# A fused four-layer kernel: five of 32 scan products on another engine, a third home for the states, paired router products

## The chip, the cores and the metric

The kernel is one program on one core of a Trainium2 chip. The metric is the device time in microseconds (us) of one execution. Before the change it was 1005.11 us, the median of three runs (1002.9 to 1006.55). The profiled execution took 1004.66 us.

## The reference

A residual stream `x` of 1024 tokens by 256 features passes eight blocks, each added with a gate. The first is a selective state space model on the context; the fourth and the eighth are mixtures of experts with a router in front.

```python
# block 1: per batch, 256 channels e, 16 states n
u = silu(conv(in_proj_w @ ctx) + conv_b)
delta = softplus(dt_proj_w @ dt_lo + dt_proj_b);  A = -exp(A_log)
def step(state, (d_t, B_t, C_t, u_t)):
    dA = exp(d_t[..., None] * A)
    state = state * dA + (d_t * u_t)[..., None] * B_t[:, None, :]
    return state, einsum('ben,bn->be', state, C_t)
y = (ys + D * u) * silu(z)                     # z = layernorm(x)
x = x + tanh(g0) * y
x = x + tanh(g1) * ffn_ternary_weights_int8_activations(layernorm(x))
x = x + tanh(g2) * attention_16_heads(layernorm(x), ctx)
x = x + tanh(g3) * moe(layernorm(x))           # logits = x @ gate_w.T, top 4 of 16, and a shared expert
x = x + tanh(g4) * map_attention;  x = x + tanh(g5) * hadamard_ffn
x = x + tanh(g6) * map_attention;  x = x + tanh(g7) * moe   # top 2 of 8
```

## The kernel before

The tokens are worked on as two halves of 512 (`HALF`), half `h` being batches 2h and 2h+1. The program is written out by hand for each engine, in the order `ORDER = ["M", "F0", "A1", "F"]`: the state space block, the quantised feed-forward block, the attention with 16 heads for each half, and then the three last feed-forward blocks with the two map attentions woven in between (tables of places, `beside`). Engines meet at semaphores, each named after what it counts.

**The scan.** There are 32 rounds `g`, one per state (16) and half (2). A round needs, for 256 channels (two groups `e` of 128) and 512 tokens:

- ScalarE copies the broadcast row B from PSUM to one of three tiles `m_Bs` (`copy_B`, L889) and makes dA = exp(delta * A) into PSUM banks 6 and 7, one exponential for each `e` (L1002). The exponential of `e` waits for the scan of the round before that read the bank. The copy of B for round g+2 stands between the two exponentials of round g.
- GpSimd makes dBu = du * B (L2057), into one of two tiles.
- VectorE runs the scan itself, state * dA + dBu, once for each `e` (L1480), and writes it into a state tile (`hst`, two tiles: `m_h` and `m_inv`). Then it makes the product with C for the round before (L1486), from the state tile and PSUM bank 3 into one of two tiles `m_hC`.
- TensorE broadcasts B (L466, bank 2) and C (L494, bank 3) from a split row, and sums the products into y, banks 0 and 1, by products with the identity (L500, four matrix instructions for a round). In TensorE's queue a round reads: B for g+3; the wait for product g-1; C for g; the sums of product g-1; in some rounds a product of value weights (L511, rounds 0, 2, ... 14 and 22 to 29).

So the next C is asked for once the last product is read, the next B stands behind the sums, and the second exponential behind the copy of B. Further work is dropped into chosen rounds: the rounding of quantised weights on ScalarE (`ROUND_AT`), the gate of half 0 at round 17 (`gated(0)`, L1466), the residual at 20 (L1351), statistics at 21 (L1315 to L1329), scales at 24 (L1520), maxima at 27 (L1511), rounded values at 30 (L1526) on VectorE, and three steps on delta of half 1 on GpSimd behind rounds 3, 6 and 9 (`delta1`).

**The end of the scan.** TensorE's queue ends with C for round 31, the sums of product 30, eight transposes of the quantised rows (L531), the sums of product 31, and the first gate and up products of the next block (L557). Their result goes through Silu on ScalarE (L1072) to VectorE (L1555).

**The router.** The activations and the router's weights are each kept as a high and a low part (`x_norm_T_hi`, `x_norm_T_lo`, `r_w_hi`, `r_w_lo`). `mm3` (L434 to L436) adds three products: high by high, high by low, low by high. `router_logits` calls it for each tile of 128 tokens (4 per half) and each half of the features (2), with the activations as the weights that are loaded and 32 columns of router weights passing. It runs for two blocks and two halves. VectorE takes the logits with one copy (L1614).

## Time and profile before

| | before |
|---|---|
| median of three runs | 1005.11 us |
| the profiled execution | 1004.66 us |
| its span in the profile | 1002.9 us |
| TensorE (PE) busy | 912.1 us, 91% |
| VectorE (DVE) busy | 715.4 us, 71% |
| ScalarE (ACT) busy | 642.6 us, 64% |
| GpSimd (POOL) busy | 492.7 us, 49% |

The span is the time from the first to the last instruction in the profile, and the busy times are shares of it. They are averages over stages: in the page's 40 slices VectorE is at 9 tenths in the second to sixth slice, and TensorE from the eleventh on. The page also gives the clock that TensorE was granted, in tenths of full speed (PEclk), slice by slice.

In the names of the profile a state tile `m_inv` is the second home of the states, and `m_split` a tile that splits the rows of B and C before the scan. Numbers behind tile names are left out in the profile, and stand in the listings of order below.

### The profile page before, as it was taken

What the parts mean: (1) busy time and instruction counts of PE and PEld (TensorE: products, weight loads), DVE (VectorE), ACT (ScalarE), POOL (GpSimd) and SP (SyncE); (2) the same over time, 40 slices, a digit from 0 to 9 for tenths busy, and PEclk for the clock granted to TensorE, in tenths of its full rate; (3) what the DMA queues carried; (4) which work ended last, traced back from release to release, by engine and by line L of the source; (5) the groups of instructions that cost most, each with busy time, mean ns of one, the idle gap of its engine ahead of it and who ended that gap; (6) DMA issues with size and microseconds to landing.
All of it is one profiled execution on the core that took longest, in us unless ns stands there. A gap on an engine that the chain in (4) does not pass through costs nothing.

```text
span 1002.9 us, 15717 instructions
## 1 busy us (share of the span) xinstructions
PE 912.1 (91%) x5336; PEld 747.2 (75%) x5336; DVE 715.4 (71%) x1303; ACT 642.6 (64%) x1246; POOL 492.7 (49%) x488
## 2 busy tenths in 40 slices
PE   6477677668999999999989999999999999999998
PEld 2133233346999999999968888888888888888887
DVE  6899998986777777777667675796666655666544
ACT  5767765766777777777655666756667544554553
POOL 1487561126766666666443443454344544444442
PEclk8599989798999999999999999999999999999999
DMA  9200100003000000000019511211112500021221
GB/s 346 115 1 0 63 1 0 1 1 159 1 2 2 1 1 1 1 2 1 1 51 339 181 53 46 61 64 54 46 58 56 232 1 1 1 74 53 62 65 45
DMA packets 17612, 56.26 MB, mean 56 GB/s; under 512 B 3073, under 2 KB 4201, under 8 KB 15389
## 3 DMA queue, kind: packets, MB, share of 16 engines
q1 hardware_dynamic: 5341, 34.27, 9.0%
q10 hardware_dynamic: 12192, 20.98, 7.1%
q8 instruction: 44, 0.72, 0.3%
q14 instruction: 35, 0.29, 0.1%
HBM read 54.08 MB, written 1.16 MB: 55 GB/s over the span
## 4 chain that ended last, share of the span: by engine, by line
PE 50%; DVE 13%; POOL 8%; issue 7%; ACT 3%; ACTq 1%; DMA 1%; DVEq 0%; POOLq 0%
PE psum L434 14%; PE psum L436 14%; PE psum L435 14%; POOL a_P L2020 3%; DVE a_max L1718 2%; POOL a_rk L1941 2%; POOL a_rq L1949 2%; DVE psum L1654 1%; PE psum L843 1%; DVE psum L1854 1%; PE psum L769 1%; PE psum L700 1%; DVE bn_st L1315 1%; PE psum L803 1%; ACT L1133 1%
## 5 line engine op out<-in xcount | busy, mean ns | idle before, releaser
L434 PE MATMUL psum<-x_norm_T_hi,f_wgu_hi 128*128 128x512 f32 x400 | 160.3, 401 | 3.2 <-DVE f_h_lo L1861 3.2
L436 PE MATMUL psum<-x_norm_T_hi,f_wgu_lo 128*128 128x512 f32 x400 | 157.5, 394 | 0.0
L435 PE MATMUL psum<-x_norm_T_lo,f_wgu_hi 128*128 128x512 f32 x400 | 156.8, 392 | 0.0
L434 PE MATMUL psum<-f_wd_hi,f_h_hi 128*128 128x256 f32 x400 | 121.9, 305 | 0.1
L1654 DVE TENSOR_TENSOR psum<-f_silu,psum 128x512 f32<-128x512 f32 x100 | 69.3, 693 | 69.5 <-PE psum L436 47.2
L436 PE MATMUL psum<-f_wd_hi,f_h_lo 128*128 128x256 f32 x400 | 112.9, 282 | 0.0
L435 PE MATMUL psum<-f_wd_lo,f_h_hi 128*128 128x256 f32 x400 | 112.9, 282 | 0.0
L1861 DVE TENSOR_TENSOR f_h_lo<-psum,f_h_hi 128x512 fp32r<-128x512 f32 x100 | 68.9, 689 | 51.6 <-ACT f_h_hi L889 51.1
L1954 POOL TENSOR_TENSOR f_wgu_lo<-f_w,f_wgu_hi 128x512 fp32r<-128x512 f32 x44 | 56.7, 1290 | 94.3 <-ACT f_wgu_hi L889 94.3
L1954 POOL TENSOR_TENSOR f_wgu_lo<-f_wb,f_wgu_hi 128x512 fp32r<-128x512 f32 x36 | 46.6, 1293 | 103.5 <-ACT f_wgu_hi L889 103.5
L2057 POOL TENSOR_TENSOR m_dBu<-m_du,m_Bs 128x1024 f32<-128x1024 f32 x31 | 73.0, 2355 | 35.1 <-DVE m_inv L1480 16.1
L2020 POOL TENSOR_TENSOR a_P<-a_P,a_row_inv 128x1024 f32<-128x1024 f32 x32 | 60.6, 1894 | 59.6 <-DVE a_row_inv L1755 59.6
L434 PEld LDWEIGHTS psum<-x_norm_T_hi,f_wgu_hi 128*128 128x128 f32 x400 | 75.6, 189 | 17.4 <-issue 3.9
L436 PEld LDWEIGHTS psum<-x_norm_T_hi,f_wgu_lo 128*128 128x128 f32 x400 | 75.0, 188 | 17.2
L435 PEld LDWEIGHTS psum<-x_norm_T_lo,f_wgu_hi 128*128 128x128 f32 x400 | 75.7, 189 | 13.2
L1133 ACT ACTIVATE f_silu<-psum 128x512 f32<-128x512 f32 x100 | 59.7, 597 | 38.5 <-PE psum L436 38.3
L434 PEld LDWEIGHTS psum<-f_wd_hi,f_h_hi 128*128 128x128 f32 x400 | 76.0, 190 | 5.3 <-issue 2.2
L435 PEld LDWEIGHTS psum<-f_wd_lo,f_h_hi 128*128 128x128 f32 x400 | 76.2, 191 | 4.6 <-issue 1.9
L436 PEld LDWEIGHTS psum<-f_wd_hi,f_h_lo 128*128 128x128 f32 x400 | 76.2, 190 | 0.0
L889 ACT ACTIVATE a_PT_hi<-psum 128x1024 fp32r<-128x1024 f32 x32 | 32.8, 1025 | 62.1 <-PE psum L769 62.1
L889 ACT ACTIVATE f_h_hi<-psum 128x512 fp32r<-128x512 f32 x100 | 58.7, 587 | 19.9 <-DVE psum L1854 19.8
L1228 ACT ACTIVATE a_P<-psum,a_neg_max,a_rq 128x256 f32<-128x256 f32 x128 | 70.7, 574 | 0.4 <-DVE a_neg_max L1722 0.4
(328 smaller groups left out, 2635.1 us busy)
## 6 DMA issues: line engine op xcount, KB each, us to landing
f_cw<-r_rows ACTq DMA_DIRECT2D x38, 256.0 KB, 3.3
f_wb<-in_f1b SPq DMA_DIRECT2D x6, 1152.0 KB, 9.7
f_w<-in_f3w SPq DMA_DIRECT2D x1, 5376.0 KB, 16.6
f_wa<-in_f1a SPq DMA_DIRECT2D x1, 3840.0 KB, 11.8
w_raw<-in_w0raw SPq DMA_DIRECT2D x1, 3072.0 KB, 14.9
f_w<-in_f2w SPq DMA_DIRECT2D x2, 1536.0 KB, 8.6
f_cw<-r_rows ACTq DMA_DIRECT2D x12, 224.0 KB, 3.0
f_cw<-r_rows ACTq DMA_DIRECT2D x12, 192.0 KB, 2.9
```

What stands on the lines that cost most here:

```text
L434: mm(out, wh, xh, start=start, stop=False, **kw)
L435: mm(out, wh, xl, start=False, stop=False, **kw)
L436: return mm(out, wl, xh, start=False, stop=stop, **kw)
L889: return A(out_, in_, ACT.Copy)
L1133: A(sg[g % 2][:, :], ps[:, 2 + 2 * (g % 2), :], ACT.Silu).then_inc(S("f_sg"), 1)
L1228: last = A(Pm[i % 2][:, t, :], ps[:, 2 + t // 2, (t % 2) * DM:(t % 2 + 1) * DM], ACT.Exp, bias=nb[:, t:t + 1], scale=rq[i % 2][:, t:t + 1] ...
L1654: V.tensor_tensor(ps[:, 2 + 2 * (g % 2), :], sg[g % 2][:, :], ps[:, 3 + 2 * (g % 2), :], ALU.mult).then_inc(S("f_m"), 1)
L1718: link(V.tensor_reduce(mx[:, :], ps[:, 2:4, :].rearrange("p a (b n) -> p (a b) n", b=2), AX, ALU.max))
L1861: V.tensor_tensor(hl[g % 2][:, :], ps[:, 2 + 2 * (g % 2), :], hh[g % 2][:, :].bitcast(f32), ALU.subtract).then_inc(S("f_hl"), 1)
L1954: G.tensor_tensor(wgl[g % 2][:, :], raw_w(l, j)[:, 0:GU], wgh[g % 2][:, :].bitcast(f32), ALU.subtract).then_inc(S("f_wg"), 1)
L2020: G.tensor_tensor(Pm[i % 2][:, :, :], Pm[i % 2][:, :, :], bc(ri[:, :].unsqueeze(2), [P, TH, DM]), ALU.mult).then_inc(S("a_pn"), 1)
L2057: G.tensor_tensor(dBu[g % 2][:, :, :], du[g // NS][:, :, :], bc(Bs[g % 3][:, :].unsqueeze(1), [P, 2, HALF]), ALU.mult).then_inc(S("m_dBu"), 1)
```

## The change

Four things change.

1. The states get a third tile, `m_split`, which is free during the scan. Round g uses tile g % 3 up to round 28, and after that two tiles in turn, since the quantised rows are written over `m_split` in round 30. The scan of round g waits for product g-3, where it waited for product g-2.
2. In rounds 10, 13, 16, 19 and 22 GpSimd makes the product with C, behind the dBu of two rounds later. It can't read the PSUM bank, so ScalarE copies C to a tile (`m_tap_w`) in those rounds. VectorE skips these products. TensorE and the scans wait for the right count of both engines' products (`products_done`).
3. The end of the scan: the transposes of the quantised rows stand before the wait for product 30 in TensorE's queue, and ScalarE issues a Silu on one element behind the copy of the transposes, so that the table is loaded there.
4. The router: high and low parts of the weights lie side by side, so that one product of 64 columns gives high by high and high by low, and a second of 32 columns adds low by high. VectorE adds the two parts of the logits in two instructions.

Beside these the `delta1` steps stand behind rounds 3, 5 and 7, and `ROUND_AT` names other rounds.

```diff
-    hst = [hst0, zinv]
+    hst = [hst0, zinv, spl]
+    POOL_ROUNDS = (10, 13, 16, 19, 22)
+    Cs = tapw.rearrange("p a b -> p (a b)")
+    def products_done(eng, n):
+        by_pool = sum(1 for r in POOL_ROUNDS if r < n)
+        if n > by_pool:
+            eng.wait_ge(S("m_hC"), n - by_pool)
+        if by_pool:
+            eng.wait_ge(S("m_hC_pool"), by_pool)
+    LAST_OF_THREE = NS + 12
+    def state_home(g):
+        return g % 3 if g <= LAST_OF_THREE else (g + 1) % 2
...
+                if g == NS + 15:
+                    loaded(pe, "identb")
+                    pe.wait_ge(S("wvo_copied"), HEADS - 1)
+                    quantised_inputs(0)
                 if g:
-                    pe.wait_ge(S("m_hC"), g)
+                    products_done(pe, g)
...
-                    last = mm3(ps[:, 7, t * 32:(t + 1) * 32], xh[:, c, sl], xl[:, c, sl], wrh[:, c, :], wrl[:, c, :],
-                               c == 0, c == KC - 1)
+                    mm(ps[:, 7, t * 64:(t + 1) * 64], xh[:, c, sl], wrs[:, c, :, :].rearrange("p a n -> p (a n)"), start=c == 0, stop=False,
+                       skip_group_check=True)
+                    last = mm(ps[:, 7, t * 64:t * 64 + 32], xl[:, c, sl], wrs[:, c, 0, :], start=False, stop=c == KC - 1, skip_group_check=True)
...
-            ROUND_AT = [9, 11, 13, 15] + list(range(17, 25))
+            ROUND_AT = [9, 10, 12, 13, 15, 16, 18, 19, 21, 22, 24, 25]
...
+                if g - 1 in POOL_ROUNDS:
+                    if g - 1 > POOL_ROUNDS[0]:
+                        act.wait_ge(S("m_hC_pool"), POOL_ROUNDS.index(g - 1))
+                    act.wait_ge(S("m_C"), g)
+                    copy(Cs[:, :], ps[:, 3, :]).then_inc(S("m_Ccopy"), 1)
...
             quantised_inputs(0)
+            A(scratch[:, 22:23], epsc[:, :], ACT.Silu)
...
-                    if g >= 2:
-                        dve.wait_ge(S("m_hC"), g - 1)
+                    if g >= 3:
+                        products_done(dve, g - 1 if g > LAST_OF_THREE else g - 2)
...
-                        V.tensor_tensor_scan(hst[g % 2][:, e, :], ps[:, 6 + e, :], dBu[g % 2][:, e, :], 0.0, ALU.mult, ALU.add).then_inc(S("m_h"), 1)
-                if g:
+                        V.tensor_tensor_scan(hst[state_home(g)][:, e, :], ps[:, 6 + e, :], dBu[g % 2][:, e, :], 0.0, ALU.mult, ALU.add).then_inc(S("m_h"), 1)
+                if g and g - 1 not in POOL_ROUNDS:
...
-            V.tensor_copy(rl[:, :, 0:nl], ps[:, 7, 0:TH * 32].rearrange("p (t n) -> p t n", t=TH)[:, :, 0:nl]).then_inc(S("b7_free"), 1)
+            parts_ = ps[:, 7, 0:TH * 64].rearrange("p (t n) -> p t n", t=TH)
+            link(V.tensor_copy(rl[:, :, 0:nl], parts_[:, :, 32:32 + nl]))
+            V.tensor_tensor(rl[:, :, 0:nl], parts_[:, :, 0:nl], rl[:, :, 0:nl], ALU.add).then_inc(S("b7_free"), 1)
...
-                    if g in (3, 6, 9):
-                        delta1(g // 3 - 1)
+                    if g in (3, 5, 7):
+                        delta1((g - 3) // 2)
+                    r = g - 2
+                    if r in POOL_ROUNDS:
+                        pool.wait_ge(S("m_h"), 2 * (r + 1))
+                        pool.wait_ge(S("m_y"), r - 1)
+                        pool.wait_ge(S("m_Ccopy"), POOL_ROUNDS.index(r) + 1)
+                        G.tensor_tensor(hC[r % 2][:, :, :], hst[state_home(r)][:, :, :], bc(Cs[:, :].unsqueeze(1), [P, 2, HALF]),
+                                        ALU.mult).then_inc(S("m_hC_pool"), 1)
```

In the listings of the program's order a line names the instruction, its output and inputs; a scan reads SCALAR_TENSOR_TENSOR with the state tile as its output. GpSimd's queue from the dBu of round 10 on, before:

```order
L2057 TENSOR_TENSOR m_dBu0_116<-m_du0_113,m_Bs1_119 128x1024 [waits m_h,m_du,m_Bcopy]
L2057 TENSOR_TENSOR m_dBu1_117<-m_du0_113,m_Bs2_120 128x1024 [waits m_h,m_du,m_Bcopy]
L2057 TENSOR_TENSOR m_dBu0_116<-m_du0_113,m_Bs0_118 128x1024 [waits m_h,m_du,m_Bcopy]
L2057 TENSOR_TENSOR m_dBu1_117<-m_du0_113,m_Bs1_119 128x1024 [waits m_h,m_du,m_Bcopy]
L2057 TENSOR_TENSOR m_dBu0_116<-m_du0_113,m_Bs2_120 128x1024 [waits m_h,m_du,m_Bcopy]
```

and in the changed kernel:

```order
L2085 TENSOR_TENSOR m_dBu0_115<-m_du0_112,m_Bs1_118 128x1024 [waits m_h,m_du,m_Bcopy]
L2085 TENSOR_TENSOR m_dBu1_116<-m_du0_112,m_Bs2_119 128x1024 [waits m_h,m_du,m_Bcopy]
L2085 TENSOR_TENSOR m_dBu0_115<-m_du0_112,m_Bs0_117 128x1024 [waits m_h,m_du,m_Bcopy]
L2094 TENSOR_TENSOR m_hC0_121<-m_inv1_125,m_tap_w_156 128x1024 [waits m_Ccopy,m_y,m_h]
L2085 TENSOR_TENSOR m_dBu1_116<-m_du0_112,m_Bs1_118 128x1024 [waits m_h,m_du,m_Bcopy]
L2085 TENSOR_TENSOR m_dBu0_115<-m_du0_112,m_Bs2_119 128x1024 [waits m_h,m_du,m_Bcopy]
L2085 TENSOR_TENSOR m_dBu1_116<-m_du0_112,m_Bs0_117 128x1024 [waits m_h,m_du,m_Bcopy]
L2094 TENSOR_TENSOR m_hC1_122<-m_inv1_125,m_tap_w_156 128x1024 [waits m_Ccopy,m_y,m_h]
```

A product with C now stands behind the dBu of round 12 and again behind that of round 15. VectorE's queue from the scans of round 15 to those of round 18, before:

```order
L1480 SCALAR_TENSOR_TENSOR m_inv1_126<-psum,m_dBu1_117 128x512 x2
L1486 TENSOR_TENSOR m_hC0_122<-m_h_121,psum 128x1024
L1480 SCALAR_TENSOR_TENSOR m_h_121<-psum,m_dBu0_116 128x512 x2
L1486 TENSOR_TENSOR m_hC1_123<-m_inv1_126,psum 128x1024
L1480 SCALAR_TENSOR_TENSOR m_inv1_126<-psum,m_dBu1_117 128x512 x2
L1486 TENSOR_TENSOR m_hC0_122<-m_h_121,psum 128x1024
L1466 TENSOR_TENSOR m_u0_111<-psum,x_norm0_50 128x512 x2
L1480 SCALAR_TENSOR_TENSOR m_h_121<-psum,m_dBu0_116 128x512 x2
```

and in the changed kernel, from the scans of round 16 on:

```order
L1506 SCALAR_TENSOR_TENSOR m_inv1_125<-psum,m_dBu0_115 128x512 x2
L1512 TENSOR_TENSOR m_hC1_122<-m_h_120,psum 128x1024
L1506 SCALAR_TENSOR_TENSOR m_split_109<-psum,m_dBu1_116 128x512 x2
L1492 TENSOR_TENSOR m_u0_110<-psum,x_norm0_50 128x512 x2
L1506 SCALAR_TENSOR_TENSOR m_h_120<-psum,m_dBu0_115 128x512 x2
```

The product of round 16 is gone from between the scans of round 17 and the gate, and three tiles take turns. TensorE's queue at the end of the scan, before, from C for round 30 to the first gate product:

```order
L494 MATMUL psum<-m_bc_split1_125,sel_bc_152 128x512
L500 MATMUL psum<-m_hC1_123,ident_f_60 128x512 x2
L494 MATMUL psum<-m_bc_split1_125,sel_bc_152 128x512
L500 MATMUL psum<-m_hC0_122,ident_f_60 128x512 x2
L531 MATMUL psum<-ident_b_61,q_x0_134 128x128 x8
L500 MATMUL psum<-m_hC1_123,ident_f_60 128x512 x2
L557 MATMUL psum<-w0_quant0_147,q_xT0_137 128x512 x2
```

and in the changed kernel:

```order
L517 MATMUL psum<-m_bc_split1_124,sel_bc_152 128x512
L523 MATMUL psum<-m_hC1_122,ident_f_60 128x512 x2
L550 MATMUL psum<-ident_b_61,q_x0_133 128x128 x8
L517 MATMUL psum<-m_bc_split1_124,sel_bc_152 128x512
L523 MATMUL psum<-m_hC0_121,ident_f_60 128x512 x2
L523 MATMUL psum<-m_hC1_122,ident_f_60 128x512 x2
L576 MATMUL psum<-w0_quant0_146,q_xT0_136 128x512 x2
```

The eight transposes moved ahead of the last C; the sums of products 30 and 31 follow each other.

## Rows read from the trace of the kernel before

**Rows 1.** Busy time by stage: start:end, length, then PE, PEld, DVE, ACT, POOL, PEclk.
```profile
47.00:165.00 118.00, 84.70 (x221) 36.06 (x221) 113.33 (x115) 80.47 (x129) 76.44 (x34) 0.93 0.04 14
...
258.00:525.00 267.00, 261.53 (x1977) 247.38 (x1976) 189.47 (x334) 195.13 (x483) 170.30 (x205) 1.00 0.02 5
525.00:1003.00 478.00, 468.69 (x2683) 406.19 (x2682) 302.88 (x630) 274.56 (x490) 202.76 (x203) 1.00 0.24 79
```

**Rows 2.** Timeline of VectorE in the scan: start, length, instruction.
```profile
88.70 2.34 DVE L1480 TENSOR_TENSOR_SCAN m_inv<-psum,m_dBu 128x512 f32<-128x512 f32 x2
90.96 1.20 DVE L1486 TENSOR_TENSOR m_hC<-m_h,psum 128x1024 f32<-128x1024 f32 x1
92.24 2.34 DVE L1480 TENSOR_TENSOR_SCAN m_h<-psum,m_dBu 128x512 f32<-128x512 f32 x2
...
105.12 1.20 DVE L1486 TENSOR_TENSOR m_hC<-m_h,psum 128x1024 f32<-128x1024 f32 x1
106.23 1.28 DVE L1466 TENSOR_TENSOR m_u<-psum,x_norm 128x512 f32<-128x512 f32 x2
```

**Rows 3.** Timeline of TensorE, the same round: from the end of product 11 on.
```profile
88.67 0.39 PE L494 MATMUL psum<-m_bc_split,sel_bc 96*128 96x512 bf16 x1 [1.21 <-DVE m_hC L1486]
88.90 1.88 PE L500 MATMUL psum<-m_hC,ident_f 128*128 128x512 f32 x4
90.61 0.59 PE L511 MATMUL psum<-a_wo,a_wvT 128*128 128x256 f32 x2
91.05 0.38 PE L466 MATMUL psum<-m_bc_split,sel_bc 96*128 96x512 bf16 x1
```

**Rows 4.** Timeline of ScalarE, the same round.
```profile
91.46 0.60 ACT L889 ACTIVATE m_Bs<-psum 128x512 f32<-128x512 f32 x1 [0.75 <-PE psum L466]
91.96 0.68 ACT L1002 ACTIVATE psum<-m_delta,neg_A 128x510 f32<-128x510 f32 x1
```

**Rows 5.** Timeline of GpSimd, one dBu of that round.
```profile
91.21 2.36 POOL L2057 TENSOR_TENSOR m_dBu<-m_du,m_Bs 128x1024 f32<-128x1024 f32 x1 [1.18 <-DVE m_inv L1480]
```

**Rows 6.** Timelines and one window around a stretch at the half level.
```profile
140.72 0.39 PE L494 MATMUL psum<-m_bc_split,sel_bc 96*128 96x512 bf16 x1 [2.10 <-DVE m_hC L1486]
140.95 3.35 PE L500 MATMUL psum<-m_hC,ident_f 128*128 128x512 f32 x4
...
142.00:144.00 2.00, 2.00 (x3) 0.67 (x2) 2.00 (x2) 0.69 (x1) 0.81 (x2) 0.50 0.00 0
...
146.42 1.22 DVE L1480 TENSOR_TENSOR_SCAN m_inv<-psum,m_dBu 128x512 f32<-128x512 f32 x1 [0.90 <-ACT psum L1002]
```

**Rows 7.** Timelines of VectorE and GpSimd around a four-element copy.
```profile
135.72 1.52 DVE L1520 COPY m_z_scale<-rstd 128x4 f32<-128x4 f32 x1
...
134.86 2.35 POOL L2057 TENSOR_TENSOR m_dBu<-m_du,m_Bs 128x1024 f32<-128x1024 f32 x1 [1.19 <-DVE m_h L1480]
```

**Rows 8.** Chain that ended last, at the loop's end: start, length, what.
```profile
167.37 0.45 PE psum L531 x8
...
170.10 1.28 ACT L1072
...
172.20 0.52 DVE q_h L1555
```

**Rows 9.** Timeline of VectorE, the gate behind the loop.
```profile
169.62 1.29 DVE L1466 TENSOR_TENSOR m_u<-psum,x_norm 128x512 f32<-128x512 f32 x2 [2.66 <-PE psum L500]
```

**Rows 10.** Timeline of TensorE at the last router products and behind them.
```profile
929.01 0.26 PE L434 MATMUL psum<-r_w_hi,x_norm_T_hi 128*128 128x32 f32 x1
929.12 0.26 PE L435 MATMUL psum<-r_w_lo,x_norm_T_hi 128*128 128x32 f32 x1
...
930.45 0.28 PE L434 MATMUL psum<-f_wd_hi,f_h_hi 128*128 128x256 f32 x1
930.57 0.28 PE L435 MATMUL psum<-f_wd_lo,f_h_hi 128*128 128x256 f32 x1
```

**Rows 11.** Instructions on the tile of the logits.
```profile
L1614 DVE COPY r_logits<-psum x3: 183/192/231, 541.4 to 930.3; 128x32 f32<-128x32 f32 x2, 128x68 f32<-128x68 f32 x1
```

More of the change, by code:

```diff
@@ L82, in flamingo_kernel @@
     gqk = place("fixed", "g_qk", [P, 1])
-    wrh, wrl = (place("fixed", f"r_w_{n}", [P, KC, 32], f32r) for n in ("hi", "lo"))
+    wrs = place("fixed", "r_w_parts", [P, KC, 2, 32], f32r)
+    wrh, wrl = wrs[:, :, 0, :], wrs[:, :, 1, :]
     bst = place("fixed", "bn_st", [P, TH, 6])
@@ L151, in flamingo_kernel @@
     w0q = [place("W0", f"w0_quant{i}", [P, KC * I0], bf16) for i in range(3)]
+    at["Wi"] = at["W0"] - KC * I0 * 2
+    inverse1 = place("Wi", "m_inverse1", [P, 2, HALF])
     w_values = place("Wd", "w_abs_values", [P, KC * I0])
@@ L211, in flamingo_kernel @@
     SOFTPLUS = [(dA[0], dBu[0], hC[0]), (hst0, dBu[1], hC[1])]
-    INV = [dA[0], spl]
+    INV = [dA[0], inverse1]
+    Cs = tapw.rearrange("p a b -> p (a b)")
+    POOL_ROUNDS = (10, 13, 16, 19, 22)
     bc_mid = [Bs[h][0:96, 0:256].bitcast(bf16) for h in range(2)]
@@ L519, in ssm @@
                     output(0).then_inc(S("m_out"), 1)
-                if g == NS + 15:
-                    loaded(pe, "identb")
-                    pe.wait_ge(S("wvo_copied"), HEADS - 1)
-                    quantised_inputs(0)
             return output
@@ L583, in hidden_T @@
                 last.then_inc(S("q_hTp"), 1)
-            pe.wait_ge(S("m_hC"), 2 * NS)
+            products_done(pe, 2 * NS)
             pe.wait_ge(S("m_Bcopy"), 2 * NS)
@@ L1485, in ssm @@
                         dve.wait_ge(S("m_y"), g - 2)
-                    V.tensor_tensor(hC[(g - 1) % 2][:, :, :], hst[(g - 1) % 2][:, :, :], bc(ps[:, 3, :].unsqueeze(1), [P, 2, HALF]),
+                    V.tensor_tensor(hC[(g - 1) % 2][:, :, :], hst[state_home(g - 1)][:, :, :], bc(ps[:, 3, :].unsqueeze(1), [P, 2, HALF]),
                                     ALU.mult).then_inc(S("m_hC"), 1)
```

## The prediction

> **What bounds the kernel now.** I read in this order. The page's engine shares name TensorE as busiest, but an average over stages says nothing of the scan. The windows by stage do: in 47 to 165 us VectorE (third column) is busy 113.33 of 118 us, while TensorE is busy 84.70, ScalarE 80.47 and GpSimd 76.44; from 525 us on TensorE is busy 468.69 of 478 us, and in the attention stage 261.53 of 267 [rows 1]. So the scan is bound by VectorE and the last stages by TensorE, and a piece of work taken from the wrong one buys nothing.
>
> Then VectorE's own timeline. A round is two scans, 2.26 us from the first's start to the product's, and a product that takes 1.20; the next scan starts 1.28 after the product did: 88.70 to 92.24 is 3.54 us. Where the instruction behind a product does not need it, it starts after 1.11 (105.12 to 106.23), so 0.17 of each round is the scan's wait for the product just issued [rows 2].
>
> Last, what the round's other engines need. From a product's end (88.62) TensorE issues C at 88.67, the sums into y at 88.90, a value product at 90.61 and the next B at 91.05 [rows 3]; ScalarE copies B at 91.46 and starts the exponential behind the copy at 91.96, 0.68 long [rows 4]. Product's end to that exponential's end is 4.02 us, 3.59 in rounds without a value product (0.43). I call this the long chain: product k is its start, and the second scan of round k+3 its end. GpSimd takes 2.36 us for a dBu and then sits idle 1.18 [rows 5]: so little is its cover, half of one more product.
>
> **The change part by part.**
>
> *Third home for the states.* The scan of round g waits for product g-3, not g-2, in rounds 3 to 28: 26 x 0.17 = 4.4 us at most. VectorE does not keep all of it: where a wait for ScalarE ends a stretch, the wait only grows by what VectorE won since the last one. Row: the second scan at 146.42 waited 0.90 behind sums that took 3.35 us [rows 6], and three shorter such waits lie in the loop. Going through the rounds one after another, 15 to 19 of the 26 count: 2.6 to 3.2 us, I take 2.7.
>
> *Five products on GpSimd.* VectorE skips 5 x 1.11 = 5.6 us. Take t0 as the end of round r's scans. GpSimd starts dBu(r+2) at t0 + 0.2 and needs 2.36 for it and 2.36 for the product [rows 5]: done at t0 + 4.9. GpSimd's work for three rounds becomes 4 x 2.36 = 9.4 us against VectorE's 3 x 3.37 - 1.11 = 9.0: it is now the tighter of the two by a little. VectorE, without the product, wants the second scan of round r+2 at t0 + 1.11 + 2.26 + 1.13 = 4.5. The long chain from product r-1, ended at t0 + 1.2, delivers at t0 + 4.8, or 5.2 with a value product: a new wait of 0.3 to 0.7. The same chain from product r delivers at t0 + 8.5 or 8.9, where VectorE wants the second scan of round r+3 at t0 + 7.9 plus the wait just had, 8.2 to 8.6: 0 to 0.7 more. So each GpSimd round keeps between 0 and 0.8 of its 1.11, nearly all of the skipped product turning into waits for the exponential. Five rounds: 0 to 4 us by this count; for the last (22) a bad case stands against it: the statistics behind product 20 leave TensorE idle long, and the sums that follow such a gap ran at half level (3.35 against 1.88 us, granted clock 0.50) [rows 3, 6], which would lengthen that chain by 1.5. I take 1.0 for all five, near the lower end, since the sum of waits is nearer to the row of 3.35 than to none. ScalarE's five copies of C (0.60 each, as its copy of B [rows 4]) lie in its idle time before the next round's first exponential; without that cover they would cost 0.5 each.
>
> *GpSimd beside VectorE's small instructions.* A four-element copy at 135.72 took 1.52 us, and ended with GpSimd's product (134.86 to 137.21) [rows 7]. The change puts 5 x 2.36 us more of GpSimd into the loop. Four small VectorE steps there can be caught (L1329, L1520, L1512, L1526); I expect the same two as before, so nothing added; bounds: -1.4 (the old one gone) to +4.7 (two more, each 2.36). The Trainium skill, SBUF — State Buffer, section "SBUF: two separate sides", says that the ports which VectorE and GpSimd share are an exclusive lock, held for a whole instruction. By that rule, the trace agrees, the copy waits to GpSimd's end, and scans and products, which read one operand from PSUM, are untouched.
>
> *The end of the loop.* The eight transposes of the quantised rows stand before the last sums, 0.45 us on the chain at 167.37 [rows 8]. Moved ahead of the wait for product 30, they run in an idle stretch of TensorE: -0.45. The Silu table is loaded at 170.10, 1.28 us on the chain, then q_sg and the first q_h at 172.20 [rows 8]. Loaded early it lies in ScalarE's idle time. What is late next: gated(1), 1.29 from 169.62 [rows 9], and the first Silu, both ready about 170.9: -1.3. Together -1.7.
>
> *Router pairs.* Between narrow products the distance is 0.111 us (929.01 to 929.12); with 256 columns it is 0.12 [rows 10]. It is hardly the columns that cost here, so I give 64 columns 0.111 too. Per token tile and half of the features three become two; 8 such per half batch, four half batches: 32 x 0.111 = 3.55. Three of them (24, 2.66 us) lie where TensorE is busy 98% of the time [rows 1]; of the first's 0.89, in the last heads of the attention stage, I count 0.6 because waits for other engines lie beside it. Sum -3.3; bounds 0 (if 64 columns cost twice 32) to -3.6. The second VectorE instruction (0.2 us, as the copy [rows 11]) hides in VectorE's idle time, 175 us in the last stages; without cover, +0.8.
>
> *At nothing:* delta1 in rounds 3, 5, 7 instead of 3, 6, 9 (needed only in round 16), the rounding of weights spread differently (same 12 instructions in ScalarE's gaps; it keeps out of the rounds with a copy of C), the new inverse buffer.
>
> **The sum.** 2.7 + 1.0 + 1.7 + 3.3 = 8.7 us, from the profiled execution's 1004.66 (span 1002.9): 996.0. The runs' median, 1005.11, lies 0.45 higher, within their spread of 3.7, so I leave it.
>
> **The rivals.**
> - *The GpSimd rounds give nothing, or take:* all five skipped products turn into waits, and round 22's chain meets the half level. For it: GpSimd's balance above. Against: the residual and statistics give the other engines time in rounds 19 to 21. Scan -1.0 only: 1004.66 - 1.0 - 1.7 - 3.3 = 998.7. Chance 0.17.
> - *The lock:* longer GpSimd work catches two more small steps, about 1.75 each, 3.5 us: 999.5. For it: GpSimd has hardly an idle moment left there. Against: of the four steps only one was caught for long before. Chance 0.07. The Trainium skill's rule on the shared ports (SBUF — State Buffer, "SBUF: two separate sides") speaks for this case.
> - *64 columns cost twice:* router 0: 999.3. Chance 0.12. For it: no row has 64 columns.
> - *The waits do not come:* third home 4.4, GpSimd rounds 4, tail 1.7, router 3.5: 991. Chance 0.10.
> - *Slower: TensorE falls to half level in the loop and stays.* Its work per round, C, sums, B (0.22 + 1.72 + 0.22), doubles to 4.3, 5.2 with a value product, over VectorE's 3.37: 22 rounds at 4.7 against 3.54 are +25, less some 10 us of VectorE's side work that it covers: 1004.66 + 15 - 5 = 1015. It decides once the idle gaps before C in GpSimd rounds grow. By the steps above the gap there is 1.1 to 1.6 us; a gap of 0.78 kept the full level, one of 2.10 did not [rows 3, 6]. Chance 0.04.
>
> **How the numbers follow.** Forecast 996.0, chance 0.50. Range 992.0 to 1000.0: it takes in the router's and the GpSimd rounds' bounds and all rivals but the slow one and the outer part of the free one. A difference of 0.3% (3 us) is about what a measurement can tell: faster needs under 1002.1. All cases but the slow one end there by themselves; two or more of the bad ones together would end within 0.3%. So 0.07 for the same, 0.05 slower (0.04, and 0.01 for more of the bad ones at once), 0.88 faster.
>
> **What would show it.** VectorE: scans 3.37 apart in undisturbed rounds; waits for ScalarE (L1002's exponential) of 0.3 to 0.7 in the second scan two rounds after 10, 13, 16, 19, 22. GpSimd: products of 2.36 us and nearly no idle time between 80 and 130 us. Scan loop's end about 3.7 us earlier, first q_h about 5.4 earlier (172.20 to 166.8), the same lead up to the attention stage, 8.7 at the end. Wrong if narrow products stand 0.16 apart or more, if the granted clock in 80 to 130 us lies well under the old one, or if the lead at 167 us is under 2.

## The result, and the profile after

| | before | after |
|---|---|---|
| median, each of four runs | 1004.94 us (1002.9 to 1006.55) | 996.83 us (995.19 to 997.09) |
| ratio, 95% interval | | 0.9917 (0.9904 to 0.993) |
| profiled execution | 1004.66 us | 996.82 us |
| its span | 1002.9 us | 995.0 us |

The change takes 8.1 us off the medians and 7.8 us off the profiled executions. The forecast was 996.0 and a gain of 8.7.

The same landmarks in both traces say where the gain lies (start in us; lead is before minus after):

| | before | after | lead |
|---|---|---|---|
| scans of round 31 | 161.75 | 157.85 | 3.90 |
| first q_h | 172.20 | 166.51 | 5.69 |
| GpSimd's first product on `a_P` (attention) | 240.87 | 236.43 | 4.44 |
| GpSimd's last product on `a_P` | 508.81 | 504.14 | 4.67 |
| first router product behind the attention stage | 537.20 | 531.97 | 5.23 |
| VectorE's first instruction on the last router logits | 930.3 | 922.9 | 7.4 |
| span | 1002.9 | 995.0 | 7.8 |

First the windows by stage, with columns as in [rows 1]: start:end, length, PE, PEld, DVE, ACT, POOL, PEclk.

```profile
47.00:160.00 113.00, 84.29 (x229) 36.98 (x229) 105.45 (x109) 82.17 (x134) 87.72 (x39) 0.93 0.04 15
253.00:520.00 267.00, 262.55 (x1971) 248.40 (x1970) 190.50 (x335) 195.96 (x485) 170.92 (x206) 0.99 0.02 5
520.00:996.00 476.00, 466.00 (x2660) 403.60 (x2658) 303.05 (x633) 274.37 (x490) 203.04 (x204) 1.00 0.24 79
```

VectorE was idle for 4.7 of 118 us in the scan; now it is idle for 7.5 of 113, and GpSimd is busy 11 us longer. The third window has 23 fewer matrix instructions in records (24 went).

VectorE's timeline after, answering to [rows 2]: the undisturbed rounds 10 and 11, then round 12, in front of which product 10 is left to GpSimd.

```profile
76.96 2.33 DVE L1506 TENSOR_TENSOR_SCAN m_inv<-psum,m_dBu 128x512 f32<-128x512 f32 x2
79.20 1.20 DVE L1512 TENSOR_TENSOR m_hC<-m_h,psum 128x1024 f32<-128x1024 f32 x1
80.32 2.33 DVE L1506 TENSOR_TENSOR_SCAN m_split<-psum,m_dBu 128x512 f32<-128x512 f32 x2
82.56 1.20 DVE L1506 TENSOR_TENSOR_SCAN m_h<-psum,m_dBu 128x512 f32<-128x512 f32 x1
84.46 1.22 DVE L1506 TENSOR_TENSOR_SCAN m_h<-psum,m_dBu 128x512 f32<-128x512 f32 x1 [0.70 <-ACT psum L1022]
```

Rounds stand 80.32 - 76.96 = 3.36 us apart, where they stood 3.54 apart. Product 10 is missing in front of the scan at 82.56, and the second scan of round 12 waits 0.70 us for its exponential. GpSimd's timeline of the same stretch, answering to [rows 5]:

```profile
79.46 2.35 POOL L2085 TENSOR_TENSOR m_dBu<-m_du,m_Bs 128x1024 f32<-128x1024 f32 x1 [1.00 <-DVE m_inv L1506]
81.77 2.34 POOL L2094 TENSOR_TENSOR m_hC<-m_inv,m_tap_w 128x1024 f32<-128x1024 f32 x1
84.08 4.67 POOL L2085 TENSOR_TENSOR m_dBu<-m_du,m_Bs 128x1024 f32<-128x1024 f32 x2
```

The product costs 2.34 us, directly behind its dBu, and the next two dBu follow without a gap. TensorE's timeline, answering to [rows 3] and [rows 6], once for product 10 and once for product 21, where GpSimd's product 22 follows:

```profile
84.26 0.38 PE L517 MATMUL psum<-m_bc_split,sel_bc 96*128 96x512 bf16 x1 [1.05 <-POOL m_hC L2094]
84.48 1.88 PE L523 MATMUL psum<-m_hC,ident_f 128*128 128x512 f32 x4
...
124.38 0.61 PE L517 MATMUL psum<-m_bc_split,sel_bc 96*128 96x512 bf16 x1 [3.06 <-DVE m_hC L1512]
124.78 3.62 PE L523 MATMUL psum<-m_hC,ident_f 128*128 128x512 f32 x4
128.20 1.06 PE L534 MATMUL psum<-a_wo,a_wvT 128*128 128x256 f32 x2
129.05 0.63 PE L485 MATMUL psum<-m_bc_split,sel_bc 96*128 96x512 bf16 x1
...
138.19 0.39 PE L517 MATMUL psum<-m_bc_split,sel_bc 96*128 96x512 bf16 x1 [2.11 <-DVE m_hC L1512]
138.42 1.88 PE L523 MATMUL psum<-m_hC,ident_f 128*128 128x512 f32 x4
```

The gap of 1.05 leaves the sums at 1.88 us. Behind the gap of 3.06 (the residual and the statistics keep VectorE) everything is slow: sums 3.62, value product 1.06 for 0.59, B 0.63 for 0.38. The window 124 to 128 us has a granted clock of 0.50, the lower of the two levels (1.2 GHz); the text calls it the half level. VectorE pays for it in round 24, and then meets the four-element copy of [rows 7]:

```profile
130.93 1.22 DVE L1506 TENSOR_TENSOR_SCAN m_h<-psum,m_dBu 128x512 f32<-128x512 f32 x1 [3.24 <-ACT psum L1022]
...
133.18 1.53 DVE L1546 COPY m_z_scale<-rstd 128x4 f32<-128x4 f32 x1
```

The end of the loop, all engines, answering to [rows 8, 9]:

```profile
159.34 0.61 PE L550 MATMUL psum<-ident_b,q_x 128*128 128x128 bf16 x8
161.03 1.28 ACT L1049 ACT_TABLE_LOAD   x1
161.35 0.39 PE L517 MATMUL psum<-m_bc_split,sel_bc 96*128 96x512 bf16 x1 [1.41 <-DVE m_hC L1512]
161.58 3.60 PE L523 MATMUL psum<-m_hC,ident_f 128*128 128x512 f32 x8
165.22 1.29 DVE L1492 TENSOR_TENSOR m_u<-psum,x_norm 128x512 f32<-128x512 f32 x2 [2.16 <-PE psum L523]
166.51 1.56 DVE L1581 SCALAR_TENSOR_TENSOR q_h<-psum,q_scales,q_sg 128x512 f32<-128x512 f32 x2
```

Transposes and table load lie in idle stretches; q_h starts as the gate ends, 8.66 us behind the scans of round 31 (10.45 before). Last, the router, answering to [rows 10]:

```profile
921.74 0.28 PE L665 MATMUL psum<-r_w_parts,x_norm_T_hi 128*128 128x64 f32 x1
921.85 0.26 PE L667 MATMUL psum<-r_w_parts,x_norm_T_lo 128*128 128x32 f32 x1
921.96 0.28 PE L665 MATMUL psum<-r_w_parts,x_norm_T_hi 128*128 128x64 f32 x1
922.07 0.26 PE L667 MATMUL psum<-r_w_parts,x_norm_T_lo 128*128 128x32 f32 x1
922.18 0.36 PE L453 MATMUL psum<-f_wd_hi,f_h_hi 128*128 128x256 f32 x1
```

The distance from a product of 64 columns to the next is 0.11 us, as it is from one of 32. VectorE's two instructions on the logits, answering to [rows 11], take 0.19 us each (ns, smallest, median and largest, then first and last start):

```profile
L1641 DVE COPY r_logits<-psum x3: 179/192/231, 535.3 to 922.9; 128x32 f32<-128x32 f32 x2, 128x68 f32<-128x68 f32 x1
L1642 DVE TENSOR_TENSOR r_logits<-psum,r_logits x3: 192/192/234, 535.6 to 923.1; 128x32 f32<-128x32 f32 x2, 128x68 f32<-128x68 f32 x1
```

### The profile page after: what moved, and what is told of

Read it like the earlier page. It is cut to its first block, busy times and chain, and to the rows that moved or that the text cites. A ratio compares the mean times of both kernels' runs of the same rounds, so it can differ in the third digit from the quotient of the medians.

```text
span 995.0 us, 15707 instructions
## 1 busy us (share of the span) xinstructions
PE 909.8 (91%) x5304; PEld 746.2 (75%) x5304; DVE 710.0 (71%) x1302; ACT 644.8 (65%) x1252; POOL 504.4 (51%) x493
## 3 DMA queue, kind: packets, MB, share of 16 engines
HBM read 54.08 MB, written 1.16 MB: 56 GB/s over the span
## 4 chain that ended last, share of the span: by engine, by line
PE 51%; DVE 13%; POOL 8%; issue 7%; ACT 3%; ACTq 1%; DMA 1%; DVEq 0%; POOLq 0%
PE psum L453 14%; PE psum L455 14%; PE psum L454 14%; POOL a_P L2048 3%; DVE a_max L1746 2%; POOL a_rk L1969 2%; POOL a_rq L1977 2%; DVE psum L1682 1%; PE psum L863 1%; PE psum L789 1%; DVE psum L1882 1%; PE psum L720 1%; DVE bn_st L1341 1%; PE psum L823 1%; ACT L1159 1%
```

## The experiments

The kernel before ran beside each group of them: 1004.93 us beside the first four, 1004.59 beside the next four, 1005.54 beside the last three. Ratios are to these. The versions that take one part alone keep the changed kernel's places of `delta1` and of the rounding of weights (`ROUND_AT`), so no run shows what these places alone are worth.

### The parts one by one

**Without GpSimd's products.** The changed kernel, with all 32 products on VectorE.

```diff
-    POOL_ROUNDS = (10, 13, 16, 19, 22)
+    POOL_ROUNDS = ()
```

> The changed kernel with no product on GpSimd (all 32 on VectorE); third home, end of the loop and router pairs stay. The changed kernel started its last scans 3.9 us earlier than the kernel before (157.85 against 161.75). Theory 1 (the skipped products turn nearly all into waits for the exponential; the third home carries the scan's gain): last scans at 158.5 to 159.5, the whole 0.5 to 1.5 us slower than the changed kernel, ratio to before about 0.993. Rival (the five skipped products carry the gain, 5 x 1.11): last scans at 161 or later, whole about 1001 us.

Measured: 998.07 us (995.59 to 999.57), ratio 0.9929 (0.9914 to 0.9944). The five products are worth 998.07 - 996.83 = 1.24 us by the medians, though the intervals of the two ratios overlap.

**The third home alone.**

```diff
+    hst = [hst0, zinv, spl]
...
+        return g % 3 if g <= LAST_OF_THREE else (g + 1) % 2
```

with POOL_ROUNDS empty, the order at the loop's end, the table and the router as before.

> The kernel before with the third home of the states alone. Theory 1: last scans 2.5 to 3.0 us earlier than before, rounds without a wait 3.36 us apart instead of 3.54, whole 2.5 us faster (ratio 0.9975). Rival: under 1 us, since another wait takes the place of the self-wait.

Measured: 1002.24 us (1001.88 to 1003.86), ratio 0.9976 (0.9966 to 0.9986): 2.69 us. Round 31 starts at 159.27, and the span is 1000.2; the lead of 2.5 us is kept to the end (2.7 in the span).

**The router alone.** Two homes, no GpSimd products, the old end of the loop; weights side by side, products of 64 and 32 columns.

> The kernel before with the router pairs alone. Theory: 24 fewer products in the stages where TensorE is full, 0.111 us each, 2.7 us, and up to 0.9 more in the attention stage: whole 2.7 to 3.6 us faster (ratio 0.9965 to 0.9973), the scan as before. Rival (the changed kernel's lead grew by 3.2 us from 513 us on for another reason, such as where its stages fell against loads): 1 us or less.

Measured: 1001.21 us (999.86 to 1001.79), ratio 0.9958 (0.9946 to 0.9971): 3.72 us. In the last stages TensorE's lead over the kernel before grows by 0.44 to 0.50 us at each router call on one half of the features (four products less, 4 x 0.111 = 0.44): 1.13, 1.57, 2.07, 2.52, 3.01, 3.45. The attention stage gave 0.9, and 0.6 came between it and the first of these calls, where the third home alone gained 0.3. The profiled execution had started with a loss of its own: four products of 512 columns behind the gate of half 0 ran at half level (3.38 us from 107.65), the second scan of round 19 waited 2.25 us where it waits 0.55 in the kernel before, and the first q_h came 0.77 us later, by nothing that the edit does.

**The end of the loop alone.** Transposes ahead of the wait for product 30, and the early Silu.

```diff
+                if g == NS + 15:
+                    quantised_inputs(0)
                 if g:
...
+            A(scratch[:, 22:23], epsc[:, :], ACT.Silu)
```

> The kernel before with the end of the loop alone (transposes ahead of the wait for product 30, early Silu table). Theory: the first q_h 1.7 us earlier (170.5 instead of 172.20), and some of it lost by 210 us, where the changed kernel's lead was 4.9 after 5.7: whole 1 to 1.7 us faster. Rival: the gate of half 1 is late instead and the first q_h gains under 0.7.

Measured: 1004.23 us (1002.88 to 1006.16), ratio 0.9992 (0.9984 to 1.0001): 0.70 us, not told from nothing. Its first q_h is 1.87 us earlier, as forecast, and GpSimd's first product on `a_P` only 0.7 earlier. So 1.2 us are lost again between them, in the quantised feed-forward block and the start of the attention stage.

The four parts add to 1.24 + 2.69 + 3.72 + 0.70 = 8.35, the whole is 8.11.

### Inside the scan

**Four products on GpSimd, not round 22.**

```diff
-    POOL_ROUNDS = (10, 13, 16, 19, 22)
+    POOL_ROUNDS = (10, 13, 16, 19)
```

> The changed kernel with four GpSimd rounds (10, 13, 16, 19), product 22 on VectorE again. In the changed kernel the second scan of round 24 waited 3.24 us for its exponential, behind sums that ran 3.62 us at the half level. Theory 1 (that product costs more than it saves, since the sums before it run at the half level): the wait falls under 1.5 us and round 22 no longer loses: last scans within 0.7 us of the changed kernel's 157.85, whole within 0.5 us. Rival (each GpSimd product saves about the same): last scans 0.5 us or more later and the whole kernel 0.5 to 1 us slower.

Measured: 997.66 us (996.38 to 997.76), ratio 0.9923 (0.9909 to 0.9936). Even with its long wait, product 22 did no harm: without it round 31 starts at 158.92 and the wait of round 24 is 1.17, but that of round 27 (1.26) is back. Round 31 is 1.07 us later than in the changed kernel, and 0.39 later with the difference of round 4 taken away (table below), so the run doesn't tell the two expected cases apart.

**GpSimd's products with two homes.** The changed kernel, states in g % 2, the scan waiting for product g-2.

```diff
-        return g % 3 if g <= LAST_OF_THREE else (g + 1) % 2
+        return g % 2
```

> The changed kernel with two homes for the states (g % 2, the scan of round g waits for product g-2), the five GpSimd rounds stay. Theory: a GpSimd product ends 4.9 us after its round's scans, and the scan two rounds on, wanted 3.4 us after them, now waits for it: 1.5 us at each of the five rounds, which eats the 1.11 saved; with the 0.17 per round lost too, last scans at 161 to 162.5, whole 3 to 4.5 us slower than the changed kernel (ratio about 0.996 to before). Rival (the third home matters only through the 0.17 per round): last scans at 160 to 160.8.

Measured: 1001.1 us (999.28 to 1001.13), ratio 0.9956 (0.9943 to 0.9968). Round 31 starts at 161.83: no gain at all in the loop. VectorE's timeline in rounds 12 and 24:

```profile
85.42 2.34 DVE L1506 TENSOR_TENSOR_SCAN m_h<-psum,m_dBu 128x512 f32<-128x512 f32 x2 [1.50 <-POOL m_hC L2094]
...
132.01 1.23 DVE L1506 TENSOR_TENSOR_SCAN m_h<-psum,m_dBu 128x512 f32<-128x512 f32 x1 [1.64 <-POOL m_hC L2094]
134.55 1.22 DVE L1506 TENSOR_TENSOR_SCAN m_h<-psum,m_dBu 128x512 f32<-128x512 f32 x1 [1.31 <-ACT psum L1022]
```

The scan of r+2 wants the tile that GpSimd still reads. The products on GpSimd need the third home; the two parts are not independent, as my sum had them.

**TensorE kept busy before round 22's wait.** In round 22 twenty bf16 products of 256 columns whose result nothing reads stand before TensorE's wait for product 21. They add work only.

```diff
+    FILL = {NS + 6: 20}
...
+                if g in FILL and g >= NS + 6:
+                    pe.wait_ge(S("m_res"), 1)
...
+                for _ in range(FILL.get(g, 0)):
+                    mm(ps[:, 4 if g == NS + 12 else 5, 256:512], sel_bc[:, 0, :], bcs[1][:, 0:256], start=True, stop=True, skip_group_check=True)
```

> The changed kernel with 20 products of 256 columns that nobody reads, on TensorE ahead of its wait in round 22, where it sat idle 3.06 us. Theory 1 (the 3.24 us wait of round 24 comes from the half level that followed the idle time): the sums behind it take 1.88 instead of 3.62, the wait of round 24 falls to 0.7 to 1.3, last scans 1.5 to 2.5 us earlier than 157.85. Rival (the wait is the GpSimd product's own lateness): it stays above 2.5 and nothing moves.

Measured: 994.29 us (993.34 to 995.34), ratio 0.9892 (0.9879 to 0.9906): by the medians 2.5 us better than the changed kernel, though the two intervals just touch. In the traces round 31 starts 1.40 us earlier, 2.04 with the difference of round 4 taken away (table below). TensorE's timeline:

```profile
121.78 2.34 PE L520 MATMUL psum<-m_bc_split,sel_bc 96*128 96x256 bf16 x20
125.00 0.39 PE L524 MATMUL psum<-m_bc_split,sel_bc 96*128 96x512 bf16 x1 [0.88 <-DVE m_hC L1519]
125.23 1.88 PE L530 MATMUL psum<-m_hC,ident_f 128*128 128x512 f32 x4
126.95 0.59 PE L541 MATMUL psum<-a_wo,a_wvT 128*128 128x256 f32 x2
```

and VectorE's:

```profile
129.01 1.22 DVE L1513 TENSOR_TENSOR_SCAN m_h<-psum,m_dBu 128x512 f32<-128x512 f32 x1 [0.70 <-ACT psum L1029]
...
131.26 2.06 DVE L1553 COPY m_z_scale<-rstd 128x4 f32<-128x4 f32 x1
```

Sums 1.88 instead of 3.62, and the wait 0.70 instead of 3.24. So the long wait was the half level, and 0.70 is what the chain itself asks. Of the 3.24 - 0.70 = 2.54 us that the wait is shorter by, the four-element copy takes back 0.53, since it starts earlier against GpSimd's instruction; that leaves the 2.0 of the loop.

**One-element steps.** The four-element copy and the step behind it (L1546, L1547) as eight instructions on one element each.

```diff
-            V.tensor_copy(zr[h][:, :], rstd[:, :])
+            for t in range(TH):
+                V.tensor_copy(zr[h][:, t:t + 1], rstd[:, t:t + 1])
```

> The changed kernel with the four-element copy of round 24 (1.53 us, ending with GpSimd's instruction) made as four copies of one element each, and the row behind it (two SBUF inputs) as four one-element steps with a scalar operand; the same in the second use, after the scan. Theory (the wide copy waits for the ports that GpSimd holds, and steps of one element do not): the eight steps take 0.5 to 0.9 us together instead of 1.52, last scans 0.6 to 1.0 us earlier, if the exponential is not late there. Rival (the copy waited for something else, such as the row's semaphore): the first of the eight takes 1.3 us or more and nothing moves.

Measured: 995.21 us (994.04 to 995.4), ratio 0.9902 (0.9887 to 0.9917). VectorE's timeline:

```profile
132.03 0.33 DVE L1547 COPY m_z_scale<-rstd 128x1 f32<-128x1 f32 x4
132.27 0.57 DVE L1549 TENSOR_SCALAR m_z_bias<-bn_mv,rstd 128x1 f32<-128x1 f32 x4
132.76 2.33 DVE L1506 TENSOR_TENSOR_SCAN m_inv<-psum,m_dBu 128x512 f32<-128x512 f32 x2
```

and GpSimd's:

```profile
131.17 2.35 POOL L2088 TENSOR_TENSOR m_dBu<-m_du,m_Bs 128x1024 f32<-128x1024 f32 x1 [0.62 <-DVE m_h L1506]
```

Eight steps take 0.73 us in the middle of GpSimd's dBu; the two took 1.52 (133.18 to 134.70). In their second use, behind the scan, where GpSimd runs nothing, the eight take the same 0.33 and 0.57; there the two had taken 0.16 each, and the block loses 0.57 us by the edit. The other gain here (its wait in round 24 was 2.04, not 3.24) comes from a shorter half-level stretch, which the edit doesn't touch. By its interval the time isn't told from the changed kernel's.

**TensorE kept busy in round 1.** The changed kernel with 26 unread products there, for two waits at 53.79 and 56.38 us (0.70 and 0.26) behind sums of 3.44 us.

```diff
+    FILL = {1: 26}
```

> The changed kernel with only the 26 unread products in round 1, where TensorE sat idle 3.5 us before its first sums. Theory (the half level there sets the two waits of 0.70 and 0.26 us near 54 us): first sums 1.88 instead of 3.62 us, both waits gone, last scans 0.6 to 1.1 us earlier, whole 0.5 to 1 us faster. Rival (the waits come from ScalarE's sums of the weights, which stand before the exponentials there): no difference over 0.3 us.

Measured: 996.34 us (994.63 to 996.75), ratio 0.9907 (0.9892 to 0.9922). The sums take 1.88 and both waits are gone, but round 31 is only 0.54 earlier, and the time isn't told from the changed kernel's. A wait of 1.26 us has appeared at 141.97, the second scan of round 27, behind sums of 3.25 us: the 1.0 us that the changed kernel's trace wins in round 27 (below) is not won here, though the program is the same from round 2 on.

**All of it together.** Fills in rounds 1, 22, 25 and 28 (26, 20, 14, 20 products) and the one-element steps.

> The changed kernel with unread products on TensorE in its idle time at four rounds (26 in round 1, 20 in 22, 14 in 25, 20 in 28, 256 columns each) and the one-element steps in place of the four-element copy. From the single edits: round 22 gave 2.0 us, the copy 0.7 (a longer wait there, 2.06 us, is also gone), round 1 should take 0.7 to 1.1 us off the two waits near 54 us, where the first sums ran 3.62 us at the half level. Theory 1: last scans at 153.8 to 155, whole 994.3 - 2 = 991 to 992.5, ratio 0.986 to 0.988. Rival (the unread products or their waits delay the ones that count): last scans at 156 or later.

Measured: 993.93 us (993.4 to 994.4), ratio 0.9886 (0.9872 to 0.9901). It is the best version, 11.6 us under the kernel before and some 3 under the changed one, but within the interval of the one fill in round 22, and its round 31 starts at 156.11, where 153.8 to 155 was expected: the single gains did not add. In this run the 26 products of round 1 ran at the half level themselves (5.75 us, where they took 4.61 in the run above) and pushed the sums behind them, so that the wait of round 3 was 0.91:

```profile
45.36 5.75 PE L520 MATMUL psum<-m_bc_split,sel_bc 96*128 96x256 bf16 x26
50.91 0.63 PE L524 MATMUL psum<-m_bc_split,sel_bc 96*128 96x512 bf16 x1
51.34 2.12 PE L530 MATMUL psum<-m_hC,ident_f 128*128 128x512 f32 x4
```

**Six products on GpSimd.** The same with six rounds.

```diff
-    POOL_ROUNDS = (10, 13, 16, 19, 22)
+    POOL_ROUNDS = (8, 12, 16, 20, 23, 27)
...
-            ROUND_AT = [9, 10, 12, 13, 15, 16, 18, 19, 21, 22, 24, 25]
+            ROUND_AT = [10, 11, 12, 14, 15, 16, 18, 19, 20, 22, 23, 25]
```

> As e9, with GpSimd making the product in six rounds, four apart where it can be (8, 12, 16, 20, 23, 27), and the rounding of weights moved off the rounds with a copy of C. With rounds three apart GpSimd's 9.4 us per three rounds meet VectorE's 9.0, so that each product keeps 0 to 0.8 of its 1.11 us; four apart VectorE needs 12.3 and GpSimd 11.8, so one wait of 0.7 (for the chain before it) should remain and 0.4 to 0.8 be kept each time. Theory: last scans 0.5 to 1.5 us earlier than e9. Rival (each skipped product turns into the same waits wherever it stands): the same as e9 within 0.3 us.

Measured: 995.42 us (993.77 to 996.43), ratio 0.9896 (0.9879 to 0.9912). Round 31 starts at 156.47, against 156.11 with five. A sixth product gives nothing, against the 0.5 to 1.5 us expected.

### The lead, round by round

The start of the first scan of a round in the kernel before minus that in the other (us), from VectorE's timelines:

| round | no GpSimd products | four | five (after) | five, fill in 22 | five, two homes |
|---|---|---|---|---|---|
| 4 | -0.11 | -0.44 | 0.24 | -0.41 | 0.02 |
| 11 | 0.95 | 0.63 | 1.30 | 0.66 | 0.03 |
| 12 | 1.13 | 1.93 | 2.60 | 1.95 | -0.26 |
| 13 | 1.31 | 1.32 | 1.98 | 1.35 | -0.26 |
| 17 | 2.03 | 1.92 | 2.58 | 1.95 | -0.55 |
| 22 | 2.22 | 3.74 | 4.40 | 3.77 | 0.78 |
| 24 | 2.58 | 4.10 | 5.86 | 5.24 | 0.34 |
| 25 | 2.57 | 2.82 | 2.52 | 3.91 | -1.09 |
| 27 | 2.93 | 3.17 | 2.87 | 4.26 | -1.09 |
| 28 | 2.58 | 2.84 | 3.91 | 5.31 | -0.07 |
| 31 | 2.57 | 2.83 | 3.90 | 5.30 | -0.08 |

Row 4 shows a difference that no edit makes: the wait at about 54 us was 0.47 to 1.10 in the runs without a fill in round 1. To compare two columns, take their row 4 away.

The first column is the third home: 0.18 in each undisturbed round, with pauses where waits for ScalarE stand, 2.57 + 0.11 = 2.7 in all. In the third column product 10 gives 1.30 at round 12, and 0.62 of it is gone at round 13. Up to round 24 the five skipped products had won 5.86 - 2.58 - 0.35 = 2.9 over the first column; at round 25 it is all gone and 0.4 more, into the wait of 3.24. The 1.0 that is there at the end (1.33 less 0.35) comes in round 27: without GpSimd's products the second scan there waits 1.26 us, and in the changed kernel it doesn't wait. TensorE's timeline without GpSimd's products:

```profile
138.14 0.55 PE L517 MATMUL psum<-m_bc_split,sel_bc 96*128 96x512 bf16 x1 [2.11 <-DVE m_hC L1512]
138.48 3.46 PE L523 MATMUL psum<-m_hC,ident_f 128*128 128x512 f32 x4
```

The idle gap is the same as that of the changed kernel at 138.19, 2.11 us, and here the sums run at half level, there at full. So the runs don't tie the 1.0 to the GpSimd products: the wait of 1.26 stands in the run with four products and in the one with the fill in round 1 as well, and is missing in the one with two homes. It goes with the level that TensorE happened to have in round 27.

## Why the prediction was right, and where it was not

**Third home: right.** Forecast 2.7, 26 rounds with 0.17 each less what waits take. Measured 2.69 by the medians, 2.7 in the loop, in steps of 0.18.

**Five GpSimd products: the sum right, its course not.** Forecast 1.0; measured 1.24 by the medians and 1.0 in the loop. The waits forecast at the second scans of r+2 and r+3 came: 0.70 and none for r = 10, 0.24 and 0.56 for 13, none and 1.17 for 16 (1.17 is over my 0.7, but 0.73 of it stands there without these products too), none for 19, where residual and statistics give time. For 22 I had the bad case with 1.5 for the longer chain; removing it shortened the wait by 3.24 - 0.70 = 2.54, since the value product and B run slowly too, not the sums alone. So the step that was mis-sized is this one, by 1.0. It was made good by the wait of round 27, which I had counted only as a bound on the third home [rows 6] and not as one that could fall away. That is luck: the run with the fill in round 1, which shares the five products, kept that wait, and its lead of 4.44 at round 31 and 1.16 at round 4 leaves 4.44 - 2.57 - 1.27 = 0.6 by the same count. I took 1.0 as what the rounds keep of 1.11 each; in truth the changed kernel lost all of it once and won 1.0 elsewhere. Less row 4, four products gave 2.83 - 2.57 + 0.33 = 0.6 in the loop, and five with the fill 5.30 - 2.57 + 0.30 = 3.0: the free rival of 4 us for these rounds was not far off once the half level of round 22 was away.

**Third home and GpSimd products as separate terms: wrong in form.** With two homes the same five products give nothing in the loop (161.83 against 161.75). As the whole has both, the sum didn't suffer.

**The lock: right.** The copy took 1.53 us (1.52 before), the step L1538 beside another dBu took 0.28 us, as before, for 0.17 where GpSimd is idle. So the same two were held, and nothing was added. The Trainium skill, SBUF — State Buffer, section "SBUF: two separate sides", has the shared ports as an exclusive lock that either side holds for a whole instruction. The copy fits: after, it ended at 134.71, and GpSimd's dBu beside it, 2.36 us from 132.32, at 134.68. The page names as the VectorE side of the lock operations in a two-port mode or with two inputs from SBUF; the eight one-element steps ran through GpSimd's dBu, so by that rule they would be neither. No run here shows it directly.

**End of the loop: the local step right, its lasting value not.** Forecast -1.7, measured 5.69 - 3.90 = 1.79 at q_h, and q_h starts as the gate ends, as forecast. I let it last to the end; alone it gave 0.70, with an interval that reaches 1. The lead at q_h and at two steps in the attention stage, over all runs (all but the last two columns have the tail edits):

| | after | e1 | e4 | e5 | e6 | e7 | e8 | e9 | e10 | e11 | e2 | e3 |
|---|---|---|---|---|---|---|---|---|---|---|---|---|
| at first q_h | 5.69 | 4.36 | 1.86 | 4.62 | 1.71 | 7.09 | 7.63 | 7.43 | 7.07 | 6.23 | 2.49 | -0.77 |
| at ScalarE's first copy into `a_P` | 4.91 | 3.80 | 1.16 | 3.79 | 1.13 | 6.53 | 7.62 | 7.41 | 5.61 | 5.41 | 2.44 | -0.90 |
| at GpSimd's first product on `a_P` | 4.44 | 3.35 | 0.70 | 3.33 | 0.68 | 6.07 | 6.82 | 7.33 | 5.13 | 4.93 | 2.46 | -0.83 |
| lost in all | 1.3 | 1.0 | 1.2 | 1.3 | 1.0 | 1.0 | 0.8 | 0.1 | 1.9 | 1.3 | 0.0 | 0.1 |

(e1 is the kernel without GpSimd's products, e2 the third home alone, e3 the router alone, e4 the end of the loop alone, e5 four products, e6 two homes, e7 the fill in 22, e8 the one-element steps, e9 all together, e10 six products, e11 the fill in 1.) The two without the tail edits lose next to nothing, nine of the ten with them lose 0.8 to 1.9. I forecast "the same lead up to the attention stage", and that failed. The loss falls into two places, and at both TensorE has a lower granted clock than the kernel before has at the same work. The windows are the kernel before, after and the third home alone, 20 to 22 us and 48 to 52 us behind their first q_h:

```profile
192.20:194.20 2.00, 2.00 (x16) 1.18 (x15) 1.58 (x5) 1.82 (x3) 0.00 (x0) 0.95 0.00 0
186.51:188.51 2.00, 2.00 (x12) 1.21 (x11) 1.52 (x6) 1.59 (x3) 0.00 (x0) 0.50 0.00 0
189.71:191.71 2.00, 2.00 (x16) 1.18 (x15) 1.58 (x5) 1.77 (x3) 0.00 (x0) 0.92 0.00 0
...
220.20:224.20 4.00, 2.07 (x10) 1.56 (x10) 3.89 (x12) 1.89 (x4) 0.95 (x1) 1.00 0.00 0
214.51:218.51 4.00, 3.52 (x10) 2.69 (x10) 3.36 (x10) 0.58 (x2) 1.73 (x1) 0.50 0.00 0
```

In the first place the kernel before is back at the full level, and the changed one isn't: its products of 512 columns still take 0.63 us there, where they take 0.38. The granted clock of this window is 0.50 to 0.60 in the eight runs that lose 0.6 to 1.5 us up to the copy into `a_P`, and 0.89 to 1.00 in the four that lose 0.0 to 0.1 there (e2, e3, e8 and e9; in e8 and e9 the full level is back even earlier than in the kernel before, which makes good the 0.57 us that the one-element steps cost there). In the second place the first query products (`x_norm_T` by `a_w`) take 0.63 for 0.40: the clock is 0.50 to 0.58 in the nine runs that lose another 0.4 to 0.8, and 1.00 in e2, e3 and e9, which lose at most 0.1. So the lost microsecond goes with a half level that TensorE still has, or has again, when the work comes earlier: the traces show the slower products and where they stand, though no run took that level away by an edit. What sets the time of these stretches no run here shows. Such stretches come elsewhere too: e1, e6 and e7 lose another 0.6 to 0.7 in one at about 240 us.

**Router: right, a little low.** Forecast -3.3, measured 3.72 alone. The distance at 64 columns is 0.11 us, and 24 products less gave 7.83 - 5.23 = 2.6 in the last stages of the changed kernel (forecast 2.66). In the attention stage the router calls gave 0.9, alone and in the changed kernel (forecast 0.6): there the lead went from 4.42 to 5.31. But the profiled execution of the changed kernel then lost 0.64 in a half-level stretch that the kernel before hasn't at that work, so that 0.2 is left at the last product on `a_P`. The windows are after's and before's:

```profile
499.20:502.50 3.30, 3.30 (x17) 3.30 (x16) 1.57 (x3) 1.86 (x4) 0.07 (x1) 0.50 0.02 5
503.90:507.20 3.30, 2.49 (x20) 2.32 (x20) 2.22 (x4) 1.89 (x4) 0.67 (x1) 1.00 0.02 5
```

Four of the twelve changed versions have this stretch in their traces (after, e5, e10, e11), the others don't, the router alone among them. The second instruction on the logits added nothing that the total shows.

**In all**, 8.7 forecast and 8.1 measured: about 1.0 too much for the tail, 0.2 and 0.4 too little for the GpSimd rounds and the router alone, and 0.2 that the parts lose together. None of the rivals came; the half level that was to stay didn't, since the gaps in GpSimd rounds up to 19 were 1.05 to 1.49 us, about the 1.1 to 1.6 forecast, and each was followed by sums of 1.88. (The gap of 0.78 that I named beside [rows 3] is that of a round behind one with a value product; the row itself has 1.21, and it too kept the full level.) Half-level stretches that fall differently from run to run cost 0.6 to 1.7 us each in the traces (0.64 in the changed kernel at 499 us, 1.7 in the router's run in round 19), so how well a term of about 1 us comes out is partly luck.

## What to carry to other kernels

When an engine is relieved in a loop with several engines, follow the lead round by round to the end of the loop and into the next stage: here five skipped products won 5 x 1.11 = 5.6 us, gave all of it back to waits, and what lasted came from a later wait that fell away in this trace and not in every version with these products. Compare the granted clock of both kernels at the same work before calling what is lost behind the loop a cost of the edit. Before moving work to another engine, ask how long it will hold the buffers, since a slower owner needs one buffer more. And where a wait follows slow matrix products, look at the gap before them: cheap work in that gap can be worth more than the move itself.
